# Mixing the cross-attention weights on GpSimd, and a three-pass value product in self-attention

## The reference

```
# self-attention, per head
out = einsum('bhst,bhtd->bhsd', softmax(scores), v)      # the value product
# cross-attention: each projection is mixed within a head, over the 4 channels j
def interfere(x): return x + 0.1 * amp[0] * einsum('bhsdi,hij->bhsdj', x, interference)
qh, kh, vh = interfere(q @ Wq.T + bq), interfere(k @ Wk.T + bk), interfere(v @ Wv.T + bv)
```

## Time and profile before

| | us |
|---|---|
| Median of 3 runs | 3474.78 (3473.62 to 3478.42) |
| The profiled execution's own time | 3474.34 |
| Its span, first to last instruction | 3472.6 |
| PE busy | 3350.2 (96%) |
| DVE busy | 1497.5 (43%) |
| ACT busy | 1197.9 (34%) |
| POOL busy | 1165.6 (34%) |
| A weight load of 512 KB (`wraw`), issue to landing | 4.0 |
| An ACT copy of 128x1024 (L588), mean | 1.05 |
| Self-attention phase | about 11 to 2025 |

### The profile page before, as it was taken

One profiled execution on the slowest core, in us unless ns is written; L12 is line 12 of the kernel. 1 busy time (PEld: TensorE's weight loads), 2 busy tenths in 40 slices (PEclk: granted clock), 3 DMA queues, 4 the chain that ended last, 5 costly groups with the idle time before them and its releaser, 6 DMA issues. The chain is left out here.

```text
span 3472.6 us, 47345 instructions
## 1 busy us (share of the span) xinstructions
PE 3350.2 (96%) x17716; PEld 2625.2 (76%) x17716; DVE 1497.5 (43%) x2401; ACT 1197.9 (34%) x2438; POOL 1165.6 (34%) x655
## 2 busy tenths in 40 slices
PE   6999999999999999999999959999999999988999
PEld 5888887888887888888787747777777777763587
DVE  3233252232342323333232336676676666662453
ACT  3223232232232322332222125555555555550110
POOL 4435334343343443534334223333333333330000
PEclk9999999999999999999999979999999999998999
DMA  4334335333344333434323157677678767643142
GB/s 167 114 107 122 102 128 164 109 114 110 97 145 146 109 115 102 146 102 134 96 72 103 37 189 230 205 213 255 204 203 269 208 194 246 195 128 152 37 143 76
DMA packets 165186, 502.46 MB, mean 145 GB/s; under 512 B 20384, under 2 KB 20384, under 8 KB 165032
## 3 DMA queue, kind: packets, MB, share of 16 engines
q1 hardware_dynamic: 155816, 466.76, 42.5%
q10 hardware_dynamic: 9216, 33.56, 2.7%
HBM read 416.35 MB, written 83.89 MB: 144 GB/s over the span
## 5 line engine op out<-in xcount | busy, mean ns | idle before, releaser
L437 POOL TENSOR_TENSOR sa_wl<-sa_wraw,sa_wh 128x1024 fp32r<-128x1024 f32 x192 | 458.0, 2399 | 776.5 <-ACT sa_wh L588 776.5
L53 PE MATMUL sa_u<-sa_ln_xh,sa_wh 128*128 128x512 f32 x1536 | 628.0, 409 | 4.4 <-DVE sa_ln_xl L246 4.4
L54 PE MATMUL sa_u<-sa_ln_xl,sa_wh 128*128 128x512 f32 x1536 | 599.3, 390 | 0.0
L55 PE MATMUL sa_u<-sa_ln_xh,sa_wl 128*128 128x512 f32 x1536 | 598.8, 390 | 0.0
L448 POOL TENSOR_TENSOR sa_pl<-sa_praw,sa_ph 128x1024 fp32r<-128x1024 f32 x128 | 317.7, 2513 | 442.0 <-ACT sa_ph L641 442.0
L1053 POOL TENSOR_TENSOR ca_probs<-ca_probs,ca_inv 128x512 f32<-128x512 f32 x256 | 266.7, 1051 | 547.1 <-DVE ca_inv L1420 547.0
L53 PE MATMUL sa_pr<-sa_ph,sa_oh 128*128 128x512 f32 x1024 | 428.3, 418 | 0.3 <-POOL sa_pl L448 0.3
L739 DVE TENSOR_TENSOR sa_acc<-sa_pr,sa_acc 128x512 f32<-128x512 f32 x256 | 176.4, 690 | 541.2 <-PE sa_pr L55 541.2
L54 PE MATMUL sa_pr<-sa_pl,sa_oh 128*128 128x512 f32 x1024 | 400.8, 391 | 0.0
L55 PE MATMUL sa_pr<-sa_ph,sa_ol 128*128 128x512 f32 x1024 | 400.0, 391 | 0.0
L53 PEld LDWEIGHTS sa_u<-sa_ln_xh,sa_wh 128*128 128x128 f32 x1536 | 289.0, 188 | 83.3 <-issue 24.2
(11 more groups left out here) (179 smaller groups left out, 5318.5 us busy)
## 6 DMA issues: line engine op xcount, KB each, us to landing
sa_wraw<-in_wqkv SPq DMA_DIRECT2D x192, 512.0 KB, 4.0
sa_praw<-in_wproj SPq DMA_DIRECT2D x128, 512.0 KB, 3.6
ca_wh<-w_folded_hi SPq DMA_DIRECT2D x96, 512.0 KB, 5.4
ca_wl<-w_folded_lo SPq DMA_DIRECT2D x96, 512.0 KB, 6.7
ca_kstack<-k_parts SPq DMA_DIRECT2D x192, 128.0 KB, 3.4
ca_qstack<-q_parts SPq DMA_DIRECT2D x96, 256.0 KB, 5.5
ca_owraw<-in_wo SPq DMA_DIRECT2D x32, 512.0 KB, 3.7
sa_nat<-in_w_nat SPq DMA_DIRECT2D x24, 512.0 KB, 4.2
```

What stands on the lines that cost most here:

```text
L53: nc.tensor.matmul(out, ah, bh, start=(first and i == 0), stop=False)
L54: nc.tensor.matmul(out, ah, bl, start=False, stop=False)
L55: ins = nc.tensor.matmul(out, al, bh, start=False, stop=(last and i == len(parts) - 1))
L437: nc.gpsimd.tensor_tensor(wl[:, u % 3], wraw[:, u % 3], f32(wh[:, u % 3]), ALU.subtract).then_inc(w_split, 1)
```

## The change

- Fold: the tile is loaded in a turned layout (inputs on partitions, outputs along the free dimension), and POOL mixes it: for each of two heads in the tile, output channel j is the sum over i of input channel i times a coefficient, in 4 multiplications and 3 additions of 128x512 elements, so 14 instructions a tile. They stand between the weight parts of the step. ACT copies the high part in one instruction after `copy_unit(4)`, POOL subtracts for the low part, SP stores both behind the loads of the next unit weights. PE, DVE and `v_ps` have no part in it any more. The coefficients (`coef`) are set up in the constants phase, from a fourth small load.
- Value product: probabilities are transposed once on DVE into `probsT` (the buffer `masked`), ACT spreads the high parts to `diagh` in four 32-partition copies, POOL the low parts to `diagl` in four 32-partition subtractions that wait for one another. v is split to `vh` (ACT) and `vl` (DVE, new `low_v`). The product has three fp32r passes.
- Semaphores are merged in the other phases, with no change of the work there.

The core of the diff:

```
+        raw = sb("sa_raw", [P, D]); term = sb("sa_term", [P, HALF]); mixed = f32(foldl[:])
 SP step:
-                    sp.wait_ge(folded, s.m * 2 + 2)
-                    sp.dma_start(nat[:], tile_of(w_nat, s.m)).then_inc(nat_loaded, 16)
+                    sp.wait_ge(mix_steps, s.m * MIXES + MIXES)
+                    sp.dma_start(raw[:], tile_of(w_turned, s.m)).then_inc(raw_loaded, 16)
...
+                if s.steady:
+                    sp.wait_ge(fold_split, s.m + 1)
+                    sp.dma_start(tile_of(w_folded_hi, s.m), f32(foldh[:])).then_inc(fold_stored, 16)
+                    sp.dma_start(tile_of(w_folded_lo, s.m), f32(foldl[:])).then_inc(fold_stored, 16)
 POOL:
+            def mix_rows(s, h, terms):
+                done = s.m * MIXES + (MIXES + h * HEAD_MIXES)
...
+                for i in terms:
+                    if i > 1 or (i == 1 and h):
+                        pool.wait_ge(mix_steps, done + (2 * i - 1))
+                    out_rows = rows if i == 0 else term[:].rearrange("p (k n) -> p k n", k=KC)
+                    nc.gpsimd.tensor_tensor(
+                        out_rows.rearrange("p k (j d) -> p k j d", j=MS),
+                        in_rows[:, i].unsqueeze(2).broadcast_to([P, KC, MS, DK]),
+                        chunk[:, i, h].unsqueeze(1).unsqueeze(3).broadcast_to([P, KC, MS, DK]), ALU.mult
+                    ).then_inc(mix_steps, 1)
+                    if i > 0:
+                        pool.wait_ge(mix_steps, done + 2 * i)
+                        nc.gpsimd.tensor_tensor(rows, rows, term[:].rearrange("p (k n) -> p k n", k=KC), ALU.add
+                                                ).then_inc(mix_steps, 1)
+            def fold_low(s):
+                pool.wait_ge(fold_hi, s.m + 1)
+                nc.gpsimd.tensor_tensor(foldl[:], mixed, f32(foldh[:]), ALU.subtract).then_inc(fold_split, 1)
+                def low_probs():
+                    pool.wait_ge(p_split, s.m * QPG + (QPG + 2))
+                    for q in range(QUADS):
+                        rows = slice(q * QW, (q + 1) * QW)
+                        pool.wait_ge(diag_hi, s.m * QUADS + (q + 1))
+                        if q > 0:
+                            pool.wait_ge(diag_ready, s.m * QUADS + q)
+                        nc.gpsimd.tensor_tensor(diagl[rows, :, q], probsT[rows], f32(diagh[rows, :, q]), ALU.subtract
+                                                ).then_inc(diag_ready, 1)
+                    pool.wait_ge(diag_ready, s.m * QUADS + QUADS)
+                out_weights([0, 1])
+                low_probs()
+                if s.proj and s.attn:
+                    weights(s.n, 3)
+                out_weights([2, 3])
                 if s.proj:
+                    if not s.attn:
+                        weights(s.n, 3)
+                    mix_rows(s, 0, [0, 1, 2])
+                    weights(s.n, 4)
+                    mix_rows(s, 0, [3])
+                    mix_rows(s, 1, [0, 1])
+                    weights(s.n, 5)
+                    mix_rows(s, 1, [2, 3])
                 if s.nxt:
+                    weights(s.n + 1, 0)
+                    fold_low(s)
+                    weights(s.n + 1, 1)
+                    weights(s.n + 1, 2)
 PE: (fold_half and its two calls are gone)
-                    nc.tensor.matmul(o_ps[t % 2][:], v[:, mp, t], diag[:, heads].rearrange("p h q n -> p (h q n)"),
-                                     start=True, stop=True).then_inc(o_done, 1)
+                    three_passes(nc, o_ps[t % 2][:],
+                                 [(vh[:, mp, t], vl[:, mp, t], diagh[:, heads].rearrange("p h q n -> p (h q n)"),
+                                   diagl[:, heads].rearrange("p h q n -> p (h q n)"))]).then_inc(o_done, 1)
 ACT:
+                def high_fold():
+                    act.wait_ge(mix_steps, m * MIXES + 2 * MIXES)
+                    act.wait_ge(fold_stored, m * 32 + 32)
+                    nc.scalar.activation(foldh[:], mixed, ACT.Copy).then_inc(fold_hi, 1)
+                def spread_probs():
+                    act.wait_ge(soft_steps, m * SPREAD + SPREAD)
+                    for q in range(QUADS):
+                        rows = slice(q * QW, (q + 1) * QW)
+                        nc.scalar.activation(diagh[rows, :, q], probsT[rows], ACT.Copy).then_inc(diag_hi, 1)
                 copy_unit(0)
-                out_weights([2, 3])
+                out_weights([2])
+                spread_probs()
+                out_weights([3])
...
                 copy_unit(4)
-                copy_fold(1)
-                store_fold()
+                high_fold()
                 if s.norm:
                     ln.deviations(act, s.b + 1)
                 high_o(2)
 DVE:
-                    for q in range(QUADS):
-                        rows = slice(q * QW, (q + 1) * QW)
-                        nc.vector.transpose(diag[rows, :, q], probs[rows]).then_inc(diag_ready, 1)
+                    nc.vector.transpose(probsT[:].rearrange("p k n -> p (k n)"),
+                                        probs[:].rearrange("p k n -> p (k n)")).then_inc(soft_steps, 1)
                 softmax()
+                low_v()
                 low_o(0)
                 next_moments(0)
-                low_fold(0)
```

More of the change, by code:

```diff
@@ L143, in _ @@
             ins.then_inc(mix_steps, 1)
+            nc.vector.memset(same_i[:], 0.0).then_inc(mix_steps, 1)
+            dve.wait_ge(mix_steps, 6)
+            for i in range(MS):
+                ins = nc.vector.memset(same_i[:, :, i, :, i], 1.0)
+            ins.then_inc(mix_steps, 1)
+            dve.wait_ge(mix_steps, 7)
+            nc.vector.scalar_tensor_tensor(coef[:].rearrange("p c i h j -> p (c i h j)"),
+                                           coef[:].rearrange("p c i h j -> p (c i h j)"), amp01[:],
+                                           same_i[:].rearrange("p c i h j -> p (c i h j)"), ALU.mult, ALU.add)
             dve.wait_ge(bias_mixed, 1)
@@ L356, in self_attention_phase @@
         soft_steps = sem("sa_soft_steps")
-        TURNED, TOPPED, SUMMED, INVERTED, SCALED = range(1, 6)
+        TURNED, TOPPED, SUMMED, INVERTED, SCALED, SPREAD = range(1, 7)
+        diag_hi = sem("sa_diag_hi")
         diag_ready = sem("sa_diag_ready")
@@ L431, in _ @@
             pool.sem_inc(p_split, QPG)
-            nc.gpsimd.memset(diag[:], 0.0).then_inc(diag_zeroed, 1)
+            pool.sem_inc(mix_steps, MIXES)
+            nc.gpsimd.memset(f32(diagh[:]), 0.0).then_inc(diag_zeroed, 1)
+            nc.gpsimd.memset(f32(diagl[:]), 0.0).then_inc(diag_zeroed, 1)
             def weights(n, u):
@@ L442, in first_block, with out_weights @@
                     weights(0, u)
+            def mix_rows(s, h, terms):
+                if not s.steady:
+                    return
+                done = s.m * MIXES + (MIXES + h * HEAD_MIXES)
+                if h == 0 and 0 in terms:
+                    pool.wait_ge(raw_loaded, s.m * 16 + 16)
+                    pool.wait_ge(fold_stored, s.m * 32 + 32)
+                chunk = coef[:, 7:8] if s.cross else coef[:, bass.ds(s.attn_g, 1)]
+                chunk = chunk.rearrange("p a i h j -> p (a i) h j")
+                rows = mixed.rearrange("p (k h n) -> p h k n", h=2, n=P // 2)[:, h]
+                in_rows = raw[:].rearrange("p (k h i d) -> p h i k d", h=2, i=MS, d=DK)[:, h]
+                for i in terms:
[12 more added lines that the diff above has]
+            def fold_low(s):
+                if not s.steady:
+                    return
+                pool.wait_ge(fold_hi, s.m + 1)
+                nc.gpsimd.tensor_tensor(foldl[:], mixed, f32(foldh[:]), ALU.subtract).then_inc(fold_split, 1)
             def step(s):
-                if s.attn:
-                    for h in range(QPG):
+                def out_weights(hs):
+                    if not s.attn:
+                        return
+                    for h in hs:
                         pool.wait_ge(p_hi, s.m * QPG + (h + 1))
@@ L449, in step @@
                                                 ).then_inc(p_split, 1)
-                if s.proj:
-                    for u in range(3, U):
-                        weights(s.n, u)
+                def low_probs():
+                    if not s.attn:
+                        return
+                    pool.wait_ge(diag_zeroed, 2)
+                    pool.wait_ge(p_split, s.m * QPG + (QPG + 2))
[12 more added lines that the diff above has]
+                out_weights([2, 3])
+                if s.proj:
+                    if not s.attn:
+                        weights(s.n, 3)
[5 more added lines that the diff above has]
+                    mix_rows(s, 1, [2, 3])
                 if s.nxt:
-                    for u in range(3):
-                        weights(s.n + 1, u)
+                    weights(s.n + 1, 0)
+                    fold_low(s)
+                    weights(s.n + 1, 1)
+                    weights(s.n + 1, 2)
             pipeline(pool, first_block, step)
```

(13 more changed lines are left out.)

108 lines of the change are left out of this document (50 added, 58 removed).

## The result

The changed kernel takes 3488.59 us (median of 6 runs, 3487.21 to 3490.3), the kernel before 3476.68 (6 runs): a ratio of 1.0027, 95% interval 1.0016 to 1.0037. It is slower by 0.3%; 3490 was forecast.

What follows compares the result with a forecast made beforehand. PE, busy 96% of the span, was taken to bound the kernel: 66.7 us leave it, but POOL's lateness and smaller terms (+55, +5, +15, +6, +1) make +15.3 on 3474.3, so 3490 us, own range 3472 to 3512.

Steps and rivals of the forecast that it cites:

- fold leaves PE: Self-attention steps with fold: PE loses both fold halves, 1.82 us in each of 24 folds, 43.7 us gained.
- three passes for one fp32 product: Value product on PE: three fp32r passes take 0.68 us against 0.86 for fp32; 0.18 x 128 = 23.0 us gained.
- units 3 and 4 late, 24 fold steps: Fold steps: POOL's low weight parts come late for PE, 2.3 us a step including unit 3's 0.7, +55 us.
- unit 3 late, 7 other steps: Steps with units but no fold: POOL's weight part for unit 3 comes 0.7 us late each, +5 us.
- three normalising steps: Fold steps that normalise the next block: first tile 2.8 us late, up to 2.2 more beside POOL; 5 each, +15.
- last step: Last self-attention step: no units hide POOL, so value product and projection come later after the scores, +6 us.
- constants: Constants phase: a fourth small load is waited for, +1 us (0 to 2).
- Rival B: POOL's mixing instructions are slow and the path turns to POOL, ACT and DVE; 3555 us at 1.5 each; chance 0.15.
- rival A: POOL keeps up and unit 4's weight part is in time, 3430 us, or 3459 with 1.2 late; chance 0.30.
- The spare 1.2 us before projection 2: Fold step: DVE's addition frees the projection's bank at 49.0 us, PE needs it at 50.3, so no wait.
- High part 1 slips to 29: hidden: ACT's high part 1 slips to 29 us behind later weight loads; projection 1 needs it at 38, so no cost.
- Nobody waits there: Fold's stores move from ACT to SP, behind six issues, at about 55 us of the step; no cost.

Runs made afterwards that it cites:

- f1: The changed kernel with the old value product (four DVE transpositions, one fp32 product, no low probability parts on POOL), mixing kept on POOL: 3446.46 us, ratio 0.9910.
- e4: e3 with the value product again one fp32 product, of the high parts alone; low parts still made but left out: 3475.49 us, ratio 0.9987.
- e3: e2 with ACT copying the fold's high part behind high parts 2 and 3 of the value product's result, not ahead: 3449.91 us, ratio 0.9923.
- e2: e1 with POOL also making unit 3's weight part ahead of the four low probability parts, behind the first out-weight part: 3460.80 us, ratio 0.9953.
- e1: The changed kernel with POOL making unit 4's weight part ahead of the first five mixing instructions, not behind: 3464.76 us, ratio 0.9965.
- e6: e3 with POOL's fold low part waiting for DVE's tiles in normalising steps, and ACT's high part 1 ahead of the weight copy: 3429.91 us, ratio 0.9861.

## Why the prediction was right

Term by term, in the profiled executions:

| term | predicted | measured | from |
|---|---|---|---|
| fold leaves PE | -43.7 | -43.7 | f1: 61.60 to 59.78, x 24 |
| three passes for one fp32 product | -23.0 | -23.7 | e4 against e3: 0.185 x 128 |
| units 3 and 4 late, 24 fold steps | +55 | +51.4 | 61.18 - 59.04 = 2.14 each |
| unit 3 late, 7 other steps | +5 | +5.0 | 59.75 - 59.04 = 0.71 each |
| three normalising steps | +15 | +8.4 | 68.21 - (63.26 + 2.14) = 2.8 each |
| last step | +6 | +8.0 | last mask addition to the next phase's first product, 7.3 longer, and 0.7 that its four products save |
| constants | +1 | +1.6 | start of the first mask addition, 72.02 and 73.59; 0.7 of it by PE's first product |
| loop ends | none | +3.6 | steps 8, 9, 16, 17 and 24 |
| unchanged phases | none | +4.1 | 1429.9 and 1434.0 |
| sum | +15.3 | +14.7 | 14.8 between the two spans |

- **POOL's schedule** was right nearly to a tenth: the part of unit 3 ends at 150.42 + 2.38 - 133.64 = 19.2 (19.2 predicted), that of unit 4 at 32.2 (32.4). Its prices held: 1.04 for the spread operand, 1.29 and 1.28 for full ones, also for 32 partitions. Rival B had hung on runs of 16 elements, rival A on cheap narrow operations; neither exists here. So the one price for every two-input operation, about 2.6 cycles an element, that the Trainium skill states in GPSIMD Engine Reference, "3.1 Elementwise", was rightly not followed for the multiplications; this trace disagrees with it: L484 takes 1041 ns where both operands are spread and L491 takes 1292 with two full ones of the same size.
- **Waited instructions**: 0.19 each was taken from two tiny operations. Here the gap is 0.15 between the low probability parts, 0.18 after an addition (159.58 + 1.29 to 161.05), and only 0.08 after a multiplication (158.47 + 1.03 to 159.58). So the five mixing instructions took 5.96 instead of 6.1, which is most of the difference between 2.3 and 2.14.
- **The spare 1.2 us before projection 2** was right: in the changed kernel nobody waits there in ordinary steps, and e2, which makes PE 2 us earlier, loses 0.7 there.
- **The normalising steps** were mis-sized, and one wait was denied that is there. The first tile is ready 52.8 us into the step, where 53 was forecast, and each step loses the forecast's 2.8, but not the 2.2 put on top for slower tiles. DVE's four tiles do take 5.98 instead of 2.98, more than was priced; PE waits only for the first, which takes 1.72 beside a busy POOL:

```profile
492.36 0.66 PE L241 MATMUL sa_s<-ident,sa_ln_x 128*128 128x128 f32 x4 [0.85 <-DVE sa_ln_x L233]
```

  Nor did PE lose its clock there: the granted clock is 1.00 from 484 to 511. The larger part of the 2.8 stands earlier, before projection 1, and has another cause, the loads. "High part 1 slips to 29: hidden" holds in ordinary steps (ACT waits 4.07 for the load, and the part ends at 31.2). In the normalising ones four loads of the next block stand ahead of the weights: ACT waits 10.03, the part ends at 37.2, and the addition behind it is late:

```profile
475.14 1.06 ACT L659 ACTIVATE sa_wh<-sa_wraw 128x1024 fp32r<-128x1024 f32 x1 [10.03 <-DMA sa_wraw<-in_wqkv]
479.59 0.50 PE L53 MATMUL sa_pr<-sa_ph,sa_oh 128*128 128x512 f32 x1 [1.50 <-DVE sa_acc L816]
```

  The late unit 4 covered part of this stall. As the other stalls went, the same wait in the first such step grew from 1.5 to 2.2 (e1) and 2.9 (e2), and e3's three steps are about 5 us each above e6's.
- **The last step**: the low probability parts are the path as predicted. The value product waits 15.43 after the scores, where it was 10.59, and the projection waits for POOL again: it starts 21.2 after the scores (21.5 forecast; 15.5 before). What was left out is the clock: the granted clock is 0.53 for the first 4.35 us of the projection, where the kernel before has 1.00 from 0.4 us after its start. Answers to the earlier trace rows:

```profile
2010.95 0.77 PE L53 MATMUL sa_o<-sa_diagh,sa_vh 128*128 128x512 f32 x1 [15.43 <-issue]
2015.65 0.80 PE L53 MATMUL sa_pr<-sa_ph,sa_oh 128*128 128x512 f32 x1 [1.81 <-POOL sa_pl L506]
```

- **Missed**: the loop ends. "Nobody waits there", as the prediction says of the fold's stores on SP, is true of semaphores, but the DMA engines are full where PE waits "for issue". First loop end, the kernel before, then the changed one; the DMA share in the waits is 0.40 and 0.67 before, 1.02 and 0.97 after:

```profile
569.20 0.64 PE L523 MATMUL sa_s<-sa_qT,sa_kT 128*32 128x128 f32 x16 [0.82 <-issue]
571.81 0.74 PE L523 MATMUL sa_s<-sa_qT,sa_kT 128*32 128x128 f32 x16 [1.97 <-issue]
```

```profile
572.04 0.87 PE L595 MATMUL sa_s<-sa_qT,sa_kT 128*32 128x128 f32 x17 [3.17 <-issue]
575.64 1.08 PE L595 MATMUL sa_s<-sa_qT,sa_kT 128*32 128x128 f32 x15 [2.73 <-issue]
```

- **Luck**: the late units were 4 and the normalising steps 7 too dear; the last step was 2, the loop ends and the unchanged phases 8 too cheap. That the sum fits within 1 us is luck; the two large terms are not. The stretch from the first product of cross-attention to the end took 1429.9 before and 1434.0 after, and 1430 to 1438 in the eight experiments, none of which touches it; these 4 us are not told apart from such differences between executions.

## What to carry to other kernels

Moving work to an idle engine is priced by the first deadline ahead of which it is inserted, not by the engine's busy share: POOL was 34% busy and 11 us ahead, and nine instructions put ahead of one weight part cost most of a 66 us gain on PE; two lines exchanged gave 0.6% of the kernel's time back. Put the parts that a saturated engine waits for first, in the order of their due times, and let work without a deadline fill what is behind. When a stall goes, look for those it was covering: four had to go, one by one, before the whole gain was there.

## What the runs showed that was not expected

- POOL takes as long for 32 partitions as for 128: 1283 ns for 32x512, 1290 for 128x512. Four narrow subtractions cost four times a full one; with the gaps between them this is 5.6 us of each step with attention.
- DVE's tile normalisation takes 0.8 us alone and up to 2.9 beside POOL instructions of 2.4 us: in e4 the median over 16 is 2868 ns, the least 800.
- A wait of PE of 2.8 us (e3, before projection 1) was followed by 4.9 us at a granted clock of 0.65, and one of 2.24 (e1, same place) by 4.2 us at 0.68; one of 2.49 there in e4 and one of 3.12 in e3's next such step left the clock at 1.00, as the waits of 0.45, 1.11 and 1.50 did in the changed kernel. The length of the wait alone does not tell them apart.
